# Softmax sums folded in groups of four pairs instead of three, in an attention kernel on one core

## The reference, cut to what matters

```
qkv = (h @ Wqkv.T + bqkv).reshape(B, N, num_heads, hd, 3)
energy = jnp.einsum('bhqd,bhkd->bhqk', q, k)
att = jax.nn.softmax(energy, axis=-1) / D ** 0.5
out = jnp.einsum('bhqk,bhkd->bhqd', att, v)
out = out @ Wp.T + bp
```

## Time and profile before

| | |
|---|---|
| time, median of 3 runs | 2970.34 us (2969.1 to 2972.1) |
| time of the profiled execution | 2964.47 us |
| its span | 2962.7 us |
| busy over the span: PE, DVE, ACT, POOL | 97%, 68%, 51%, 61% |
| one attention block | 48.9 us |

### The profile page before, as it was taken

The page is one execution under the profiler, slowest core; times in us unless marked ns, Lnnn a source line. Parts: engine busy times, 40 slices in busy tenths (PEclk is TensorE's granted clock), DMA queues, the critical chain, the costliest instruction groups (busy, mean ns, idle before and its releaser), DMA issues.

```text
span 2962.7 us, 41353 instructions
## 1 busy us (share of the span) xinstructions
PE 2867.7 (97%) x15018; PEld 1922.8 (65%) x15018; DVE 2008.0 (68%) x3559; ACT 1509.1 (51%) x2756; POOL 1801.8 (61%) x797
## 2 busy tenths in 40 slices
PE   4899999999999999999999999999999999999997
PEld 2787788888888887855555555555555555555456
DVE  6873322222333555778888888888888888888639
ACT  3552233232333321246666666666666666666654
POOL 2776310111110333248999999998989898898954
PEclk8899999999999999999999999999999999999999
DMA  6543100000001567475668876588866788766668
GB/s 213 179 141 129 44 21 9 29 29 29 29 15 57 189 220 224 160 196 120 141 132 178 185 154 139 129 179 170 176 131 143 148 177 175 153 134 138 162 199 300
DMA packets 155051, 405.65 MB, mean 137 GB/s; under 512 B 12101, under 2 KB 30505, under 8 KB 134342
## 3 DMA queue, kind: packets, MB, share of 16 engines
q0 software_dynamic: 22608, 164.64, 28.9%
q1 hardware_dynamic: 132248, 238.41, 25.4%
HBM read 144.51 MB, written 92.31 MB: 80 GB/s over the span
## 4 chain that ended last, share of the span: by engine, by line
PE 54%; DVE 2%; ACT 0%; DMA 0%; issue 0%; DVEq 0%; SPq 0%; ACTq 0%
PE psum L1749 18%; PE psum L1761 16%; PE psum L1734 16%; PE psum L1789 3%; PE psum L37 1%; PE psum L39 1%; PE psum L38 1%; DVE part_max L1870 1%; DVE p_h L2176 0%; DMA p_att_lo<-att_parts 0%; ACT probs L1840 0%; DVE p_stats L2182 0%; DVE p_h L2170 0%; DVE p_var L2193 0%; PE psum L1740 0%
## 5 line engine op out<-in xcount | busy, mean ns | idle before, releaser
L1870 DVE TENSOR_REDUCE part_max<-psum 128x1 f32<-128x512 f32 x1984 | 1211.7, 679 | 162.2 <-PE psum L1734 156.9
L1840 ACT ACTIVATE probs<-psum 128x512 f32<-128x512 f32 x2048 | 1042.4, 613 | 473.5 <-PE psum L1749 471.4
L1984 POOL TENSOR_TENSOR pair<-probs 128x2048 f32<-128x2048 f32 x204 | 938.6, 4603 | 139.3 <-ACT probs L1840 135.0
L1749 PE MATMUL psum<-queries,keys 128*128 128x512 f32 x2048 | 838.2, 411 | 7.5 <-PEq L2380 3.1
L1734 PE MATMUL psum<-keys,queries 128*128 128x512 f32 x1984 | 787.6, 398 | 0.6
L1749 PEld LDWEIGHTS psum<-queries,keys 128*128 128x128 f32 x2048 | 383.4, 188 | 341.3 <-issue 213.3
L1761 PE MATMUL psum<-probs,values 128*32 128x512 f32 x4096 | 510.0, 598 | 0.0
L1081 DVE TENSOR_TENSOR h_lo<-w_stage,h_hi 128x512 fp32r<-128x512 f32 x128 | 100.8, 788 | 485.0 <-ACT h_hi L989 484.9
L1734 PEld LDWEIGHTS psum<-keys,queries 128*128 128x128 f32 x1984 | 373.8, 188 | 74.4 <-DVE part_max L1870 16.9
L982 ACT ACTIVATE w_stage<-psum,b_col 128x512 f32<-128x512 f32 x128 | 88.3, 690 | 482.2 <-PE psum L39 481.4
L1761 PEld LDWEIGHTS psum<-probs,values 128*32 128x32 f32 x4096 | 106.8, 109 | 239.4 <-issue 123.3
(11 more groups left out here) (342 smaller groups left out, 3839.8 us busy)
## 6 DMA issues: line engine op xcount, KB each, us to landing
pair<-pair POOLq DMA_DIRECT2D x94, 1024.0 KB, 7.7
raw_weight<-pair POOLq DMA_DIRECT2D x32, 1024.0 KB, 7.9
pair<-raw_weight POOLq DMA_DIRECT2D x31, 1024.0 KB, 8.0
queries<-q_parts SPq DMA_DIRECT2D x96, 256.0 KB, 6.2
keys<-k_parts SPq DMA_DIRECT2D x42, 512.0 KB, 6.5
s_x<-in_x_dram SPq DMA_DIRECT2D x8, 1024.0 KB, 7.7
s_y<-in_x_dram SPq DMA_DIRECT2D x8, 1024.0 KB, 6.1
y_rows<-s_y SPq DMA_DIRECT2D x8, 1024.0 KB, 4.8
```

The costliest lines, as they stand in the source:

```text
L1749: nc.tensor.matmul(psum[:, SC + unit % 3, :], keys[place(count)[0]][:, h, kt * P:(kt + 1) * P], queries[count % NQ][:, h, :], start=True, ...
L1840: act.activation(probs[tile % NPROB][:, h, :], psum[:, SC + unit % 3, :], ACT.Exp).then_inc(exp_ready, 1)
L1870: dve.tensor_reduce(part_max[:, h * TT + qt, kc:kc + 1], max_slot(), AX.X, ALU.max).then_inc(max_read, 1)
L1984: pool.tensor_tensor(pair[number % NPAIR][:, :, :], probs[2 * number % NPROB][:, :, :], probs[(2 * number + 1) % NPROB][:, :, :], ALU.add) ...
```

## The change

1. The groups of all blocks but the last are pairs (0,1,2,3) and (4,5,6,7): two totals and six folds to a block. `SUM_LAG` is 8 for all, so the totals stand at tile 15 of the block and at tile 7 of the next.
2. Three folds form a chain in a group. The fold into the third pair is issued in the middle of the addition of the fourth, which is cut in two halves (2 heads each); the fold into the fourth pair is issued after the addition of the first pair of the next group.
3. The six key parts after the last use of a sequence's keys are issued one at a time over two blocks (at tiles 10 and 14, then 2, 8, 11 and 14), where before they were issued at tiles 10, 11, 14, then 2, 5, 8. The values are issued after tile 5 instead of 3, two blocks on.
4. `normalise` stands before pair 7 instead of 6 (in the last block still before 6).
5. The rounding copy of the result (`att_hi`) is made on ScalarE, at tile 3 behind the exponential of head 1, not on GpSimd. For the last block but one it is made after the last exponential, where before it was made before the last block's pair 6.

```diff
-    AV_LAG, SUM_LAG, LAST_LAG = 3, 10, 8
+    AV_LAG, SUM_LAG = 3, 8
...
-              for group in (((0, 1, 2), (3, 4, 5), (6, 7)) if count < BLOCKS - 1 else ((0, 1), (2, 3), (4, 5), (6, 7)))]
+              for group in (((0, 1, 2, 3), (4, 5, 6, 7)) if count < BLOCKS - 1 else ((0, 1), (2, 3), (4, 5), (6, 7)))]
...
-                if ends(count - 1):
-                    scored(count, 2 + 3 * row)
-                    load_keys(group(count - 1) + 1, place(count - 1)[0], 1, row)
-                if row == 0 and ends(count - 2):
-                    scored(count, 3)
+                if row == 0 and ends(count - 1):
+                    scored(count, 2)
+                    load_keys(group(count - 1) + 1, place(count - 1)[0], 0, 2)
+                if row == 1 and ends(count - 2):
+                    scored(count, 5)
                     sp.wait_ge(av_ready, NKT * (count - 1))
                     load_values(group(count - 2) + 1, place(count - 2)[0])
+            if ends(count - 1):
+                scored(count, 8)
+                load_keys(group(count - 1) + 1, place(count - 1)[0], 1, 0)
             if count > 1:
                 scored(count, 9)
                 store(count - 2)
...
+        def split_high(count):
+
+            act.wait_ge(weighed, count + 1)
+            act.wait_ge(att_st, 32 * (count + 1))
+            act.activation(att_hi[:, :], att[:, :], ACT.Copy).then_inc(att_split, 1)
...
+                if count > 1 and kt == 3 and h == 1:
+                    split_high(count - 2)
...
+        split_high(BLOCKS - 2)
         copy_out(BLOCKS - 1)
+        split_high(BLOCKS - 1)
...
-            if p == 6 and count > 0:
+            if p == (7 if count < BLOCKS - 1 else 6) and count > 0:
                 normalise(count - 1)
-            if p == 6 and count == BLOCKS - 1:
-                split_result(count - 1)
...
-            pool.tensor_tensor(pair[number % NPAIR][:, :, :], probs[2 * number % NPROB][:, :, :],
-                               probs[(2 * number + 1) % NPROB][:, :, :], ALU.add).then_inc(pair_ready, 1)
-            if number in FOLDS and number - 1 not in FOLDS:
+            target, even, odd = pair[number % NPAIR], probs[2 * number % NPROB], probs[(2 * number + 1) % NPROB]
+            nth = GROUPS[OF[number]].index(number)
+            if nth == 3:
+                pool.tensor_tensor(target[:, 0:HG // 2, :], even[:, 0:HG // 2, :], odd[:, 0:HG // 2, :], ALU.add).then_inc(half_made, 1)
+                fold(number - 1)
+                pool.wait_ge(half_made, FOURS.index(OF[number]) + 1)
+                pool.tensor_tensor(target[:, HG // 2:HG, :], even[:, HG // 2:HG, :], odd[:, HG // 2:HG, :], ALU.add).then_inc(pair_ready, 1)
+            else:
+                pool.tensor_tensor(target[:, :, :], even[:, :, :], odd[:, :, :], ALU.add).then_inc(pair_ready, 1)
+            if nth == 1 and number in FOLDS:
                 fold(number)
-            if number - 1 in FOLDS and number - 2 in FOLDS:
+            if nth == 0 and number > 0 and len(GROUPS[OF[number - 1]]) == 4:
                 fold(number - 1)
+        split_result(BLOCKS - 2)
```

More of the change, by code:

```diff
@@ L1526, in attention_stage @@
     UNITS = HG * NKT
-    AV_LAG, SUM_LAG, LAST_LAG = 3, 10, 8
+    AV_LAG, SUM_LAG = 3, 8
     GROUPS = [tuple(PAIRS * count + p for p in group) for count in range(BLOCKS)
-              for group in (((0, 1, 2), (3, 4, 5), (6, 7)) if count < BLOCKS - 1 else ((0, 1), (2, 3), (4, 5), (6, 7)))]
+              for group in (((0, 1, 2, 3), (4, 5, 6, 7)) if count < BLOCKS - 1 else ((0, 1), (2, 3), (4, 5), (6, 7)))]
     DIRECT = len(GROUPS) - 2
+    FOURS = [g for g, group in enumerate(GROUPS) if len(group) == 4]
     OF = {number: g for g, group in enumerate(GROUPS) for number in group}
@@ L1562, in attention_stage @@
     inverted, spread = sem("den_inverted"), sem("inverse_spread")
-    weighed, att_split = sem("att_weighed"), sem("att_split")
+    weighed, att_split, half_made = sem("att_weighed"), sem("att_split"), sem("half_made")
     SC, MX, OUT = 0, 3, 7
@@ L1587, in fold_wait @@
         engine.wait_ge(folded[n % 2], 16 * (n // 2 + 1))
-    SUMMED_AT = {2 * group[-1] + 1 + (SUM_LAG if group[-1] < PAIRS * (BLOCKS - 1) else LAST_LAG): g for g, group in enumerate(GROUPS[:DIRECT])}
+    SUMMED_AT = {2 * group[-1] + 1 + SUM_LAG: g for g, group in enumerate(GROUPS[:DIRECT])}
     WP_AT = (BLOCKS - 1) * NKT + 3
@@ L1688, in sync @@
             if ends(count):
-                for n in range(2):
-                    scored(count, 10 + n)
-                    load_keys(g + 1, b, 0, n)
+                scored(count, 10)
+                load_keys(g + 1, b, 0, 0)
+            if ends(count - 1):
+                scored(count, 11)
+                load_keys(group(count - 1) + 1, place(count - 1)[0], 1, 1)
             if count < BLOCKS - 1:
@@ L1695, in sync @@
                 scored(count, 14)
-                load_keys(g + 1, b, 0, 2)
+                load_keys(g + 1, b, 0, 1)
+            if ends(count - 1):
+                scored(count, 14)
+                load_keys(group(count - 1) + 1, place(count - 1)[0], 1, 2)
             if count >= BLOCKS - B:
@@ L1952, in split_result @@
         def split_result(count):
-            pool.wait_ge(weighed, count + 1)
-            pool.wait_ge(att_st, 32 * (count + 1))
-            pool.tensor_copy(att_hi[:, :], att[:, :]).then_inc(att_split, 1)
             pool.wait_ge(att_split, count + 1)
```

## The result

| | before | after |
|---|---|---|
| median of 11 runs | 2971.01 us | 2977.76 us (2966.97 to 2985.27) |
| ratio to before, 95% interval | | 1.0022 (1.0012 to 1.0031) |
| profiled execution, its span | 2964.47, 2962.7 us | 2983.61, 2981.8 us |
| first to last turn of the maxima, 30 blocks | 1463.6 us | 1470.7 us |
| TensorE busy in that stretch | 1463.4 us | 1448.6 us |

The forecast was 2949.6 with a range of 2941 to 2964. The median is 28 us above it, outside the range. A stretch is still that of one execution, and where it and the median differ, both are given.

The account below looks back on a forecast made before the run. TensorE's matmuls were taken to bound the kernel, 48.9 us a block. -26.7 for totals, +5 for changes of keys and +1 for the end gave -20.7 us, from the median 2970.3 to 2949.6, range 2941 to 2964.

Parts of the forecast that it names:

- The saving: TensorE in the attention: one total of 0.86 us less in 31 blocks, 26.7 us; new block 48.0 us.
- GpSimd's load: GpSimd per block, with halved additions, six folds and no copy: 45.9 of 48.0 us, including short waits.
- the other moves: ScalarE's copy: nothing, 18 us if its cover were gone; later store and parts at the end: 0, bounds 0 and +1.5.
- The 1 us for the end: End of last block but one: loads of results, weights and rows meet folds 5 to 7; 1 us, bounds 0 and 3.
- six such changes, 0.8 us for each, 5 us together: Totals waiting for folds delayed by loads at changes of keys, values included; bounds 0 and 3.5 each, 21 us.
- The rule of service: DMA queues: work served nearly in order of arrival; a fold is delayed by what came before, hardly by what comes after.
- rival 2: DMA engines mix the queues, so parts behind a fold delay it: 6.1 us a change, 37 in all, 2981; chance 0.10.
- I walked through one change from a quiet block: Two blocks with key parts, in arrival order: only second block's fold 3 on the edge, landing 90.6 against total at 90.4.
- What a wait costs: A total waiting for a late fold holds up TensorE and all others: a late fold costs its lateness in full.
- 2.7 and 2.5 us of room: Quiet blocks: fold 3 lands at 39.7 against a total at 42.4, fold 7 at 63.8 against 66.3.
- landing times of 9.2 us on: First group's chain of folds: from a landing time of 9.2 us per fold TensorE waits; the median was 7.7.
- Rival 3: GpSimd falls behind everywhere, fold 3 0.8 us late in all 62 groups: +23 us, 2993; chance 0.05.

Follow-up runs that it names:

- experiment 2: Changed kernel with most bytes of keys and values of head groups 1 to 3 left out, so not computing the reference: 2949.93 us, ratio 0.9931.
- experiment 4: Changed kernel with groups (0,1,2), (3,4,5), (6,7) and the 10-tile lag of the kernel before, other moves kept: 2969.5 us, ratio 0.9995.
- experiment 6: Changed kernel loading only the first 128 tokens of the values of head groups 1 to 3, keys in full (small values): 2963.15 us, ratio 0.9967.
- experiment 8: Changed kernel with totals two tiles later and normalise before pair 6, plus the fourth pair's addition uncut, fold issued before it: 3005.18 us, ratio 1.011.

## Why the prediction was wrong, point by point

**The saving was right.** A total is 0.86 us; blocks are 48.0 us apart where no keys change, and experiment 2 has 26 us less in 30 blocks.

**GpSimd's load was right in quiet blocks** (44.84 us busy of 48.0, where 45.9 with waits was forecast), and that the other moves cost nothing was right (experiment 4). The 1 us for the end, with a bound of 3, was too small: TensorE waited 5.9 us there, for a fold again, in a chain that met four transfers of 1024 KB.

**The step that failed is the term "six such changes, 0.8 us for each, 5 us together".** It measured 33 in the profiled execution and 27 by the medians, above its bound of 21 either way. With the medians' 27 and the 5.9 of the end the sum is -26.7 + 27 + 5.9 = +6, and the medians are 6.8 apart. Three parts of the term were wrong.

1. *The rule of service.* From the earlier trace rows I took it that a transfer issued behind a fold does not delay it. In the changed kernel a key part was issued at 1665.78, 0.5 us behind a fold, and that fold took 11.2 us to land. In 1667 to 1671, while both were on their way, the DMA queues of the changed kernel read:

```profile
q1 hardware_dynamic: 124, 0.47, 48.7%
q0 software_dynamic: 42, 0.34, 42.3%
```

   From 1666 to 1668.7 all packets were those of SP's queue (77, 0.32 MB); then both queues' moved side by side. The Trainium skill ("DMA: Bandwidth & Descriptors", Queues, rings and completion order) lets an engine take turns between its queues packet by packet; the second half of this window agrees with it, and the one that I had read before it does not.

   My own rows had a second such case. GpSimd in the kernel before, and then the DMA queues in 1982.2 to 1984.4, with all that moved packets:

```profile
1980.20 0.88 POOL L1967 DMA_DIRECT2D pair<-pair  x1 [0.30 <-POOL pair L1984]
```

```profile
q1 hardware_dynamic: 123, 0.45, 102.9%
```

   The key part of the earlier trace rows was issued at 1980.25, behind this fold, and its packets and those of the queries passed before the fold's; the fold took 11.7 us. I had read the earlier trace rows as loads that waited, and not asked what waited for them. My rival 2 stood on the mixing of the queues and had 6.1 us for each change; measured were 5.5 on average in the profiled execution and 4.6 by the medians, but unevenly (0.0 to 8.6) and largely where values and keys meet. So it was near in size, and that a load behind a fold delays it is borne out; its walk through each change is not.

2. *What meets what.* I walked through one change from a quiet block. With keys alone (experiment 6) that walk was off by 6.6 us in six changes (11.6 for 5), most of it in one. But in blocks 7, 15 and 23 the values of the change before stand in front of the first key parts of the next, and the walk never had this block; the longest wait stands there, at the total of tile 15 of block 7, behind three folds of 11.2, 11.2 and 10.0 us. The order of SP's queue over four blocks would have shown it.

3. *What a wait costs.* I put a late fold at its lateness. Between the turns TensorE is idle for 22.4 us but loses 33, the rest by slower work of the same matmuls, at half clock: the granted clock is 0.50 of 2.4 GHz in 1687 to 1692, behind the longest wait, and in 2397 to 2402, behind another. Lateness of 22 us became a loss of 33; the sum had no term for it.

**Room and chain.** I had worked out 2.7 and 2.5 us of room, and a wait from landing times of 9.2 us on. The quiet blocks bear them out: their folds took 6.9 to 9.5 us and no total waited. What I took from it was the wrong odds. A term whose bounds were 0 and 21 us, by a rule read from one window of 4 us, decided the sign, and I put it at 5.

**Rival 3** (GpSimd behind everywhere) did not happen in this kernel. In experiment 8 GpSimd is behind from the first loads on, but there it is ScalarE that waits, for pair additions, and not the totals for folds.

## What to carry to other kernels

When a chain of DMAs gets a link and its consumer comes earlier, cost the worst block, not the quiet one: list everything in the other queues over the whole period, and see which transfers come together. When the trace has a fold of 11.7 us beside 7.7 at the median, find what passed before it first. Room before a wait of the engine that sets the pace is cheap where the consumer is small; here two tiles more, which no ring objects to, turned a loss of 7 us into a gain of 13, and with one more step moved back, of 20. An addition that stands behind a wait for a DMA is worth cutting so that half of it runs ahead of the wait.

## What the runs showed of the hardware that I had not expected

- TensorE's granted clock was 0.88 in the stretch of the wait and 0.50 in the 5 us behind a wait of 5.5 us; the same two groups of matmuls took 1.94 us each, where the weighing ahead of the wait took 1.06. Over 30 blocks the busy time rose by 10.7 us beside 22.3 us of more idle time. The share is not fixed: with small values it was 2.3 us beside 8.7.
- A key part issued 0.5 us behind a fold moved most of its packets before the fold's first, and the fold landed after 11.2 us; another, issued 0.05 us behind a fold, passed ahead of it too (11.7 us). Queries issued at 1976.34, 1.9 us behind a fold whose packets were moving since 1975.8, waited for its end in the window of the earlier trace rows. These three cases would fit that a load waits only for a fold already moving; this was not tested.
- Rows of pair additions read 4.87 us where they start some 0.3 us before the row ahead of them ends, be it a DMA's issue or another addition (1668.28 behind 1665.92), and 4.60 in the kernel before: the addition ends no later.
